# Transformer block with a mixture of experts: all eight experts for every token, or the two chosen ones in blocks of 256 scattered rows

## What is computed

```python
x = x + attn(layernorm(x), Wq, bq, Wk, bk, Wv, bv, Wo, bo)   # x: 1 x 2048 x 128, 16 heads of 64, causal linear attention
xf = layernorm(x)                                            # 2048 x 128
logits = xf @ gate_w                                         # 8 experts
top_w, top_idx = top_k(logits, 2)
top_w = softmax(top_w)
combine = zeros(t, e).at[arange(t), top_idx].add(top_w)
h = gelu(einsum('td,edf->tef', xf, w1) + b1)                 # f = 512
y = einsum('tef,efd->ted', h, w2) + b2
x = x + einsum('ted,te->td', y, combine)
```

## Time and profile before

| what | value |
|---|---|
| median of 3 runs | 473.44 us (473.42 to 473.53) |
| the profiled execution | 474.08 us |
| its span | 472.3 us |
| PE busy | 457.2 us, 97% of the span |
| DVE, ACT, POOL busy | 365.6, 245.6, 89.7 us |
| moved by DMA | 19.23 MB, mean 41 GB/s |

### The profile page before, as it was taken

How to read it: one execution, slowest core, us unless ns; L and a number is a source line. 1 busy time by engine, 2 the same in 40 slices (tenths; PEclk the granted TensorE clock), 3 DMA queues, 4 the chain that set the end, 5 groups by cost and what they waited for, 6 DMA issues and landing times.

```text
span 472.3 us, 10839 instructions
## 1 busy us (share of the span) xinstructions
PE 457.2 (97%) x4241; PEld 386.9 (82%) x4241; DVE 365.6 (77%) x804; ACT 245.6 (52%) x431; POOL 89.7 (19%) x69
## 2 busy tenths in 40 slices
PE   3999999999999999999999999999999999999996
PEld 2779998788998889988889987688888888888884
DVE  5688857786857786767685568999898989889886
ACT  4662235723225722236622258386777777768771
POOL 1021111101111101220112140412232222223200
PEclk9999999999999999999999999899999999999999
DMA  8400000000000000000000013070312040202003
GB/s 259 135 2 14 8 8 1 1 1 15 8 7 2 0 3 15 8 8 1 0 4 1 3 50 129 4 219 5 131 48 89 0 155 22 89 0 89 0 0 91
DMA packets 15883, 19.23 MB, mean 41 GB/s; under 512 B 1416, under 2 KB 12992, under 8 KB 15072
## 3 DMA queue, kind: packets, MB, share of 16 engines
q1 hardware_dynamic: 15472, 17.02, 11.5%
q0 software_dynamic: 288, 1.57, 0.9%
q10 hardware_dynamic: 80, 0.02, 0.0%
HBM read 17.50 MB, written 1.11 MB: 39 GB/s over the span
## 4 chain that ended last, share of the span: by engine, by line
PE 90%; DVE 6%; DMA 2%; ACT 1%; issue 1%; POOL 0%; SPq 0%; DVEq 0%; ACTq 0%
PE ps L886 11%; PE ps L887 10%; PE ps L888 10%; PE ps L963 7%; PE ps L1001 7%; PE ps L1008 6%; PE ps L980 6%; PE ps L1036 6%; PE ps L1126 6%; PE ps L1127 6%; PE ps L1125 6%; PE ps L1028 3%; PE ps L928 3%; DVE hT_lo L804 1%; DVE am L642 1%; DMA ident<-c_ident 1%
## 5 line engine op out<-in xcount | busy, mean ns | idle before, releaser
L513 ACT ACTIVATE hT<-ps,b_now 128x512 f32<-128x512 f32 x128 | 87.6, 688 | 41.7 <-PE ps L888 40.9
L804 DVE TENSOR_TENSOR hT_lo<-hT,hT_hi 128x512 fp32r<-128x512 f32 x128 | 84.6, 699 | 1.5
L464 ACT ACTIVATE os<-ps 128x260 f32<-128x260 f32 x64 | 24.9, 389 | 105.7 <-PE ps L1008 102.5
L388 POOL TENSOR_TENSOR accT<-accT,part 128x512 f32<-128x512 f32 x28 | 40.8, 1458 | 107.7 <-DVE part L824 107.7
L353 POOL TENSOR_TENSOR on<-tcs,rden 128x1024 f32<-128x1024 f32 x16 | 30.5, 1904 | 160.3 <-DVE rden L665 160.3
L808 DVE CAST hT_hi<-hT 128x512 fp32r<-128x512 f32 x64 | 45.1, 704 | 12.1 <-ACT hT L513 11.0
L652 DVE TENSOR_TENSOR state<-ps,state 128x260 f32<-128x260 f32 x64 | 27.4, 427 | 34.4 <-ACT os L464 32.3
L886 PE MATMUL ps<-yTall,w_hi 128*128 128x512 f32 x128 | 51.4, 402 | 0.0
L887 PE MATMUL ps<-yTall,w_hi 128*128 128x512 f32 x128 | 51.2, 400 | 0.0
L888 PE MATMUL ps<-yTall,w_lo 128*128 128x512 f32 x128 | 50.9, 398 | 0.0
L1125 PE MATMUL ps<-hT_hi,w_hi 128*128 128x512 f32 x128 | 50.4, 394 | 0.0
(11 more groups left out here) (116 smaller groups left out, 846.9 us busy)
## 6 DMA issues: line engine op xcount, KB each, us to landing
comb_row<-rows SPq DMA_DIRECT2D x6, 1024.0 KB, 4.8
w_in<-in_L_ffn_w SPq DMA_DIRECT2D x16, 256.0 KB, 4.9
comb_row<-rows POOLq DMA_DIRECT2D x2, 768.0 KB, 5.0
x_sb<-in_L_attn_x SPq DMA_DIRECT2D x4, 256.0 KB, 5.5
pair<-c_pair SPq DMA_DIRECT2D x16, 64.0 KB, 2.0
out<-x_sb SPq DMA_DIRECT2D x4, 256.0 KB, 2.3
kn<-in_L_attn_Wk SPq DMA_DIRECT2D x1, 512.0 KB, 5.0
kn<-in_L_attn_Wv SPq DMA_DIRECT2D x1, 512.0 KB, 5.4
```

Source lines behind the costliest of these rows:

```text
L513: act.activation(hT[:, b, :], ps[:, b, :], ACT.Gelu, bias=b1_now[:, j * FB + b:j * FB + b + 1]).then_inc(h_ok, 1)
L804: dve.tensor_tensor(hT_lo[:, n % 2, b, :], hT[:, b, :], f32(hT_hi[:, n % 2, b, :]), ALU.subtract).then_inc(hlo_ok, 1)
```

## The change

Each token is computed for its two chosen experts only. The change builds, while the stages run, a list of rows sorted by expert in device memory. `ybuf` has 2048 places for each expert. SP first fills it with blank rows (`blank`). After the router of a stage, PE counts with a triangular matrix how many tokens ahead chose the same expert (`ranks`), DVE makes the place of each token and choice from it (`places`), and POOL scatters the tokens' rows of 130 numbers (values, destination index, weight) into `ybuf` with eight indirect DMAs (`rows_out`). `full_blocks`, `blocks_before`, `match_blocks`, `block_table` and `table` make a table `tab` on chip: for each block of TB = 256 rows its expert and its first row. NE = 5 blocks can be named before stage 3 is routed, and NB = 23 blocks in all cover every possible distribution.

A block b is loaded by `load_rows(b)` and `load_weights(b)` (rows and w1, both at addresses read from `tab` into registers), turned by `block_rows`, and goes through `hidden(b)`, Gelu, halves (`high_even` on POOL, `halves` on DVE), `down(b)` with w2 of the expert kept in SBUF (`W`), `low_part` on ACT and `weighed` on DVE. `results_out(b)` scatters the 256 result rows to `zbuf`, two rows per token. At the end SP loads `zbuf`, and DVE's `add_results` adds both rows to the residual. The high and low halves of all experts' weights are made during the first three attention stages (`weight_high` on ACT, L457 and L461 on POOL) and stored in device memory by SP. The 32 steps, `weigh`, `accT` and `turn_back` are gone.

```diff
+NE = (T * 2 * (NS - 1) // NS - E * (TB - 1) + TB - 1) // TB
+NB = (2 * T + E * (TB - 1)) // TB
...
+            sp.wait_ge(blank_in, 16 * 3)
+            for h in range(2):
+                sp.dma_start(ybuf.rearrange("(r h p) w -> p r h w", h=2, p=P)[:, :, h, :],
+                             blank[:, h, None, :].broadcast_to([P, PLACES // TB + 1, ROW])).then_inc(blank_out, 16)
...
+            def load_weights(b):
+                if b >= 3:
+                    sp.wait_ge(h_ok, (b - 2) * FB)
+                which = sp.value_load(tab[0:1, 0, b:b + 1], min_val=0, max_val=E - 1)
+                sp.dma_start(f32(w1b[b % 3][:]), w1s[bass.ds(which, 1), :, :].rearrange("e p n -> p (e n)")
+                             ).then_inc(w1_in[b % 3], 16)
+            def load_rows(b):
+                if b >= 4:
+                    sp.wait_ge(z_out[(b - 4) % 3], 32 * ((b - 4) // 3 + 1))
+                at = sp.value_load(tab[0:1, 1, b:b + 1], min_val=0, max_val=PLACES)
+                sp.dma_start(yb[b % 4][:], ybuf[bass.ds(at, TB), :].rearrange("(h p) w -> p h w", p=P)
+                             ).then_inc(yb_in[b % 4], 16)
...
+            for b in range(NE, NB):
+                load_rows(b)
+                if b + 1 < NB:
+                    load_weights(b + 1)
+            for k in range(3):
+                sp.wait_ge(z_out[k], 32 * len(range(k, NB, 3)))
+            zv = zbuf[0:2 * T, :].rearrange("(k c p) d -> p k c d", p=P, c=NC)
+            for k in range(NS):
+                for s in range(2):
+                    sp.dma_start(zin[:, s, k * SC:(k + 1) * SC, :], zv[:, s, k * SC:(k + 1) * SC, :]
...
+            def rows_out(i, m):
+                if m == 0:
+                    pool.wait_ge(rows_ok, i + 1)
+                    pool.wait_ge(slot_ok, i + 1)
+                    pool.wait_ge(wts_ok, i + 1)
+                k, c = m // SC, m % SC
+                pool.indirect_dma_start(ybuf, bass.IndirectOffsetOnAxis(ap=slot[:, k, c:c + 1], axis=0),
+                                        yr[:, k, c, :], None).then_inc(y_out[i], 16)
...
+            def high_even(b):
+                if b >= 2:
+                    pool.wait_ge(z_ps, b - 1)
+                pool.wait_ge(h_ok, b * FB + 2)
+                pool.tensor_copy(hT_hi[:, b % 2, 0:2, :], hT[:, b % 2, 0:2, :]).then_inc(hhi0_ok, 1)
+            def results_out(b):
+                pool.wait_ge(z_ok, b + 1)
+                if b >= 1:
+                    pool.wait_ge(z_out[(b - 1) % 3], 32 * ((b - 1) // 3 + 1))
+                for h in range(2):
+                    pool.indirect_dma_start(zbuf, bass.IndirectOffsetOnAxis(
+                        ap=yb[b % 4][:, h, D:D + 1].bitcast(U32), axis=0),
+                        z[:, b % 3, h, :], None).then_inc(z_out[b % 3], 16)
+            for i in range(NS):
+                attention(i)
+            high_even(0)
+            root(NS - 1)
+            high_even(1)
+            second_rows(NS - 1)
+            results_out(0)
+            high_even(2)
+            results_out(1)
+            high_even(3)
+            results_out(2)
+            for m in range(2 * SC):
+                rows_out(NS - 1, m)
+            high_even(4)
+            results_out(3)
+            results_out(4)
+            for b in range(NE, NB):
+                high_even(b)
...
+            def weight_high(a):
+                act.wait_ge(win_in[a % 2], 16 * (a // 2) + 16)
+                if a >= 2:
+                    act.wait_ge(stage_out[a % 2], 16 * (a // 2))
...
+            def low_part(b):
+                act.wait_ge(z_ps, b + 1)
+                if b >= 2:
+                    act.wait_ge(z_ok, b - 1)
+                for h in range(2):
+                    last = act.activation(zt[:, b % 2, h, :], ps[:, 4, h * TB + D:h * TB + TB], ACT.Copy,
+                                          scale=yb[b % 4][:, h, D + 1:D + 2])
+                last.then_inc(zt_ok, 1)
...
+            def halves(b):
+                if b >= 2:
+                    dve.wait_ge(z_ps, b - 1)
+                for q in range(2):
+                    if q == 1:
+                        dve.wait_ge(h_ok, b * FB + FB)
+                        dve.tensor_copy(hT_hi[:, b % 2, 2:4, :], hT[:, b % 2, 2:4, :]).then_inc(hhi1_ok, 1)
+                    dve.wait_ge(hhi1_ok if q else hhi0_ok, b + 1)
+                    dve.tensor_tensor(hT_lo[:, b % 2, 2 * q:2 * q + 2, :], hT[:, b % 2, 2 * q:2 * q + 2, :],
+                                      f32(hT_hi[:, b % 2, 2 * q:2 * q + 2, :]), ALU.subtract).then_inc(hlo_ok, 1)
+            def weighed(b):
+                dve.wait_ge(zt_ok, b + 1)
+                if b >= 3:
+                    dve.wait_ge(z_out[b % 3], 32 * (b // 3))
+                for h in range(2):
+                    last = dve.scalar_tensor_tensor(out=z[:, b % 3, h, :], in0=ps[:, 4, h * TB:h * TB + D],
+                                                    scalar=yb[b % 4][:, h, D + 1:D + 2], in1=zt[:, b % 2, h, :],
+                                                    op0=ALU.mult, op1=ALU.add)
...
+            def first_rows():
+                for b in range(2):
+                    pe.wait_ge(yb_in[b], 16)
+                    for h in range(2):
+                        last = pe.transpose(ps[:, 6, b * TB + h * P:b * TB + h * P + P], yb[b][:, h, 0:D], ident[:])
...
+            def block_rows(b):
+                pe.wait_ge(yb_in[b % 4], 16 * (b // 4) + 16)
...
+                for h in range(2):
+                    last = pe.transpose(ps[:, 5, b % 2 * TB + h * P:b % 2 * TB + h * P + P], yb[b % 4][:, h, 0:D],
+                                        ident[:])
+                last.then_inc(xb_ps, 1)
...
+            def hidden(b):
...
+                w = w1b[b % 3]
+                for f in range(FB):
+                    if f % 2 == 0 and b >= 2:
+                        pe.wait_ge(h_ok, (b - 2) * FB + f + 2)
+                    last = split3(ps[:, b % 2 * 2 + f // 2, f % 2 * TB:f % 2 * TB + TB], (0, F), (xb_hi(b), xb_lo(b)),
+                                  lambda t: w[:, t + f * P:t + f * P + P], lambda t: t)
+                    if f % 2 == 1:
+                        last.then_inc(h_ps, 1)
...
+            def down(b):
+                which = pe.value_load(tab[0:1, 0, b:b + 1], min_val=0, max_val=E - 1)
+                if b == 0:
+                    pe.wait_ge(w2_in, 16 * E)
+                if b >= 1:
+                    pe.wait_ge(z_ok, b)
+                for f in range(FB):
+                    if f % 2 == 0:
+                        pe.wait_ge(hlo_ok, 2 * b + f // 2 + 1)
+                    for h in range(2):
+                        w = W[:, bass.ds(which, 1), f * TB:f * TB + TB].rearrange("p e n -> p (e n)")
+                        mm(ps[:, 4, h * TB:h * TB + TB], hT_hi[:, b % 2, f, h * P:h * P + P], w,
+                           start=(f == 0 and h == 0), stop=(f == FB - 1), skip_group_check=True)
+                        w = W[:, bass.ds(which, 1), f * TB:f * TB + D].rearrange("p e n -> p (e n)")
+                        last = mm(ps[:, 4, h * TB + D:h * TB + TB], hT_lo[:, b % 2, f, h * P:h * P + P], w,
+                                  start=False, stop=(f == FB - 1), skip_group_check=True)
+                last.then_inc(z_ps, 1)
...
+            for b in range(NE, NB):
+                if b + 2 < NB:
+                    block_rows(b + 2)
+                if b + 1 < NB:
+                    hidden(b + 1)
+                down(b)
...
-            with pe.Fori(0, E // EJ - 1) as i:
-                for m in range(STEPS):
-                    hidden(i, m + AHEAD)
-                    down(i, m + AHEAD - 1)
```

More of the change, by code:

```diff
@@ new lines, in _ @@
+            a = 0
+            for i in range(NS - 1):
+                done = 0
+                for c in range(SC):
+                    pair_in_next(i, c)
+                    for m in range(LOW_BEFORE[c][0], min(LOW_BEFORE[c][1], W_SLOTS[i])):
+                        weight_out(a + m)
+                        if a + m + 2 < NW:
+                            weight_in(a + m + 2)
+                a += W_SLOTS[i]
+            for k in range(2):
+                sp.wait_ge(stage_out[k], 16 * E)
@@ L370, in _, with attention @@
+            def attention(i):
+                at = sum(W_SLOTS[:i])
+                if i >= 1:
+                    root(i - 1)
+                    second_rows(i - 1)
                 for c in range(SC):
-                    if c < 2:
+                    if i < NS - 1:
+                        for m in range(LOW_BEFORE[c][0], min(LOW_BEFORE[c][1], W_SLOTS[i])):
+                            weight_low(at + m)
+                    if i >= 1 and c < 2:
                         pool.wait_ge(oT_ps, (i - 1) * 2 * SC + 2 * (c + SC - 1))
+                    if i == 0 and c == 1:
+                        pool.wait_ge(tri_ok, 1)
@@ L391, in _ @@
[L391 to L398 removed]
+                    if i >= 1 and c < len(SPREAD):
+                        if i == 1 and c == 0:
```

(52 more changed lines are left out.)

670 lines of the change are left out of this document (386 added, 284 removed).

## The result

The changed kernel takes **511.71 us** (median of 4 runs, 511.23 to 516.29); the kernel before, on the same chip, 473.49. The ratio is 1.0828, 95% interval [1.0766, 1.0891]: slower by 38 us where I had forecast 9.5. The profiled execution took 512.19 us, its span is 510.4. It was measured unedited twice more beside the experiments: 514.36 (ratio 1.0855 [1.0781, 1.0928]) and 526.93 (1.1109 [1.1037, 1.118]); the second has waits on ACT that are told under c1 and c2.

A forecast was written before the change was run, and what follows sets the result against it. Before the change PE's streamed columns bound the kernel; after it, a round trip of 13.0 us per two blocks. First block at 289.6, + 70 + 104 + 18 = 481.6 us span, 483 median; range 457 to 515.

The forecast's parts named there:

- mechanism of the loop: In the block loop, PE stops being the bound; every second block waits on a round trip, 13.0 us for two blocks.
- Part 2: Blank fill on SP's queue early in the kernel: stalls ACT's weight_high(2) by 0 to 25 us, taken as 4.
- fill at half rate: Rival on the blank fill: unaligned writes take twice the time, 21 us more stall, 504 us; chance 0.08.
- ACT idle over 10 us at weight_high(2): Sign that the forecast is wrong: ACT waits this long at its third weight copy because of the fill.
- 25 us at the least: Shortest time for the blank fill, from loads that moved 1,322 packets in 2 us.
- a fifth more: The blank fill takes this much over its least time, which gives a stall of 4 us.
- Part 1: Work before the blocks: ranks, first_rows and table add 3.8 us, and PE waits 3.8 us for the first rows.
- Parts 3 to 5: From hidden(0): early blocks to the end of block 6, 70 us; blocks 7 to 22, 104; the end, 18.
- part 4: Blocks 7 to 22: eight rounds of two blocks at 13.0 us each, 104 us.
- Slow scatters: Rival in POOL's scatters: descriptor work and DVE's SBUF work block each other, 1.9 us a scatter; chance 0.13.
- Faster: Rival in the block loop: a round shorter than 11.8 us, down to 11.3, for 463 us; chance 0.36.
- the likeliest case: The forecast itself for the whole kernel: 474.5 to 497 us, chance 0.40.

The follow-up runs named there:

- c1: The changed kernel again, unedited, as control on the chip of e5 to e7: 514.36 us, ratio 1.0855 to the kernel before.
- c2: The changed kernel again, unedited, as control on the chip of e11: 526.93 us, ratio 1.1109 to the kernel before.
- e4: Changed kernel with eight row buffers, so the load of block b waits for the scatter of b-8 instead of b-4: 510.2 us, ratio 1.0735.
- e5: Changed kernel with eight row buffers and POOL's cast of the first half of the hidden activations moved to DVE: 477.48 us, ratio 1.0077.
- e3: Changed kernel with the blank fill cut into seven parts, two fifths in place, the rest between stage 0's weight transfers: 505.42 us, ratio 1.065.
- e1: Changed kernel with the same fill bytes written as 2,080 pieces of 4,160 bytes instead of 16,640 of 520: 507.54 us, ratio 1.0706.
- e2: Changed kernel with the store of the expert biases issued ahead of the fill instead of behind it: 524.97 us, ratio 1.1037.
- e6: Changed kernel with the fill spread as in e3 and ACT's triangle-constant copy moved behind stage 0's projections: 491.37 us, ratio 1.0386.
- e8: Changed kernel, still four row buffers, with only the cast of the first half of the hidden activations moved to DVE: 515.2 us, ratio 1.0891.
- e10: e7 with stage 3's last outputs ahead of the first row blocks, and rows loaded two blocks further ahead: 465.39 us, ratio 0.9831.
- e7: Changed kernel with four edits: eight buffers, cast on DVE, fill spread, triangle-constant copy late: 453.88 us, ratio 0.9581.
- e11: The kernel of e7 measured again, unedited, on the chip of c2: 466.0 us, ratio 0.9806.

## Why the prediction was right and wrong

**Direction and the mechanism of the loop: right.** PE stopped being the bound, and the round trip through POOL, HBM and SP took its place. e4 and e5 show it by taking parts of that trip away: blocks 5 to 22 take 110.3 us in the first profile, 97.1 without the wait for b-4, and 87.5 when POOL's cast is gone too. The loop came out as forecast; nearly all of the excess arose ahead of it.

**Part 2, the fill: the step that failed, and over half of the miss.** I took 4 us with bounds of 0 and 25, since I let the fill run a fifth slower than the loads of the earlier trace rows; "fill at half rate" was a rival with 0.08, and it is what happened. My sign for it, ACT idle over 10 us at weight_high(2), is in the profile. It ran at some 177 GB/s (8.65 MB from 17.6 to about 66.5), 0.6 of the 298 of the earlier trace rows, and the stall was 20.2. It moved stage 1 by 18.4 (e3, which has no stall, begins it at 78.67), 14.4 more than forecast. The step that failed is the rate behind "25 us at the least" and "a fifth more": a packet rate read from 2 us of loads was carried over to 8.65 MB of stores. The fill's first 2 us do run at 278 GB/s; what those rows could not show is that stores of such pieces don't keep it up. e1 shows that the pieces count, not the bytes (409 GB/s with 4,160-byte pieces), e2 clears the bias store, e3 shows that the same pieces stall nothing in another order. The Trainium skill (DMA: Bandwidth & Descriptors, Specifications) asks for 512 bytes or more for line rate, which 520-byte rows satisfy; the measurement decides that this is not enough here. The same page of the Trainium skill (How a descriptor splits into AXI transactions) has a reason that would fit: a piece that does not start on a 256-byte boundary is charged from the boundary below it. The trace speaks against it as the whole reason, since the same pieces start at 278 GB/s and only then fall to 153; but no run here separates alignment, length, and load against store.

**Start-up: a missing term of 4.5 us.** ACT's new copy of the triangle constants waits 5.3 us for the last small constant (it starts at 17.61), and the projection copies are queued behind it. The prediction had no term for this. With both, stage 1 is 23.2 late where I had 4: 18.4 for the stall, 4.5 for this copy (e3 to e6), and 0.3 left over.

**Part 1: too small by 7.5 us**, the second step that failed. The ranks cost 1.36 a stage instead of 0.9. In stage 3 I had 5.8 and it is 12.4: 1.26 of waiting for ex, the half clock behind it (3 us at 0.54, 1.4), 0.8 more for the first rows, 0.5 more for the ranks, and the rest, 2.6, is about the half clock behind those rows (some 4.5 us of busy matmuls, 2.3 by estimate). I had charged the clock in the blocks, not behind the waits ahead of them. The sum: 19.2 + 0.9 + 6.6 = 26.7 of the 26.8.

**Parts 3 to 5: right, part 4 with terms that cancel.** The table came 50 us behind the first block as forecast, high_even(4) at 39.9 (41 to 42), and e8 confirms that POOL's eight scatters ahead of that cast hold it (10 us). In the round of 13.15 the scatters and the landing are 4.63 (I had 3.6: from the start of the second scatter it is 3.35, where I had 1.0 + 1.6), SP and rows 2.97 (2.5), and from the rows to weighed 4.6 with no low_part (5.5 + 0.6): this way led through Gelu, POOL's cast and DVE's halves, which I had priced at 4.9 and passed over for PE at half clock. In the first profile the clock of the loop is 0.87 on average, so that choice was wrong, and that the sum still gives 13.0, with two terms too small by 1.5 and one too large by 1.5, is luck. c1, at 0.77, has rounds of 13.6. The register load's floor of about 600 ns in the Trainium skill (DMA: Bandwidth & Descriptors, Latency and other measured facts), which no row could check before, does not show as the price of the load alone: of the 0.72 between landing and issue the register load is 0.26 (393.43 to 393.70, where I had 0.3), and the rest is the arithmetic on the address and the hand-overs. The measurement decides.

**Rivals.** Slow scatters is out:

```profile
L518 POOL DMA_INDIRECT zbuf<-z,yb x46 | 44.6, 970 | 74.6 <-DVE z L1039 67.6
```

They take 970 ns each, 1.0 in the sum, and the block of POOL by DVE that this rival asked for does not show: in e10 the scatter at 381.49 takes 0.96 with a whole DVE cast (381.69 to 382.11) inside it. "Faster" needed a round under 11.8 and fell with 13.1. The range held the time (457 to 515), the likeliest case's (474.5 to 497) did not.

## What to carry to other kernels

A bulk transfer on a queue is a wait for everything issued behind it: price it by the size of its contiguous pieces, and ask who is queued behind it before asking how many bytes it has. Work that is cut by sorting comes back as a latency loop, so count how many buffers the loop spans, then look for the second ring that stands behind the first (here two engines' program orders), since lifting the first alone gave 13 of the 23 us that both gave between blocks 5 and 22, and lifting the second alone (e8) gave nothing there. Where PE is made to wait, add the slow clock behind the wait to its price, and put ready work in front of it.

## What the hardware did that I had not expected

- Stores of 520-byte rows begin at 278 GB/s and then fill the DMA engines at 153 to 186; the same bytes as 4,160-byte pieces go at 409 (e1).
- SP's issue of a store of many pieces holds SP itself: 19.3 us for the two stores of 16,640 pieces, and the next issue, of 16 KB, 26.7 us; ahead of the stores that issue takes 0.51 (e2). With an eighth of the pieces (e1) the two stores hold SP for 1.0 us and the next issue for 8.6.
- An indirect scatter of 128 rows takes POOL 0.96 us and 0.30 to the next, and lands 2.24 us after its start in quiet (end of e7), 3.9 with loads beside it (e10). From a landing to the start of a scatter that waits for it POOL needs 0.74.
- In after and e11, 256-column matmuls start every 0.117 us at full clock and every 0.213 at half. A pair of 256 and 128 columns starts every 0.23 at full clock, as long as two of 256: the 128-column one saves nothing there.
- On three of the chips the changed kernel and its variants had ACT waits marked remote, of 2.1, 0.7, 1.4 and 0.7 to 1.5 us in stages 1 and 2 (later ones too), at the same places in every kernel, and the first block came 10 us later (326.86 against 316.35); in the first measurement and on the chip of c1 there were none. At the first of these places one instruction transfer is in flight with the wait (c2) and without it (c1), so what ACT waits for is not shown.
